# The attention loop of three engines written out for sixteen heads instead of four

## The reference

```python
q = split(x @ Wq.T + bq)
k = split(x @ Wk.T + bk)
v = split(x @ Wv.T + bv)
q_stp = q @ Wqs.T + bqs
k3 = k @ Wks.T + bks
v3 = v @ Wvs.T + bvs
cross_kv = jnp.cross(k3, v3, axis=-1)
scores = (jnp.einsum('bhqd,bhkd->bhqk', q, k) + jnp.einsum('bhqc,bhkc->bhqk', q_stp, cross_kv)) * temp
attn = jax.nn.softmax(scores, axis=-1)
out = jnp.einsum('bhqk,bhkd->bhqd', attn, v)
```

## Time and profile before

| what | us |
|---|---|
| median of 3 runs | 4282.59 |
| lowest and highest | 4281.64 to 4284.22 |
| the profiled execution's own time | 4292.46 |
| its span, first to last instruction | 4290.5 |
| first part of the program | 0 to about 2370 |
| attention: first maxima to last head | 2376.5 to about 3986 |
| feed-forward net | about 3986 to 4290 |
| TensorE busy over the span | 3558.7 (83%) |
| VectorE busy | 3161.5 (74%) |
| ScalarE busy | 2212.4 (52%) |

### The profile page before, as it was taken

How to read it: one execution, slowest core, us unless ns; L and a number is a source line. 1 busy time by engine, 2 the same in 40 slices (tenths; PEclk the granted TensorE clock), 3 DMA queues, 4 the chain that set the end, 5 groups by cost and what they waited for, 6 DMA issues and landing times. The chain is left out here.

```text
span 4290.5 us, 50229 instructions
## 1 busy us (share of the span) xinstructions
PE 3558.7 (83%) x14625; PEld 1618.9 (38%) x14625; DVE 3161.5 (74%) x3753; ACT 2212.4 (52%) x3556; POOL 1513.9 (35%) x1140
## 2 busy tenths in 40 slices
PE   4228778697786987868896799999999999999898
PEld 1015435344353443534553132323222232323565
DVE  5988777887778877777512887878778787878443
ACT  4335544455444544445321277777777777777221
POOL 2977666676666766667611000000000000000110
PEclk7669889898898997988998699999999999999999
DMA  2011212212122121121210200000000000000001
GB/s 93 28 32 44 65 39 77 62 55 72 42 73 65 45 76 45 62 74 50 91 55 25 89 22 17 16 17 24 17 17 16 17 24 17 16 17 19 30 29 34
DMA packets 110769, 183.17 MB, mean 43 GB/s; under 512 B 14495, under 2 KB 84599, under 8 KB 101817
## 3 DMA queue, kind: packets, MB, share of 16 engines
q1 hardware_dynamic: 110521, 180.09, 13.4%
HBM read 153.95 MB, written 26.09 MB: 42 GB/s over the span
## 5 line engine op out<-in xcount | busy, mean ns | idle before, releaser
L1588 DVE TENSOR_REDUCE tile_max<-ps 128x1 f32<-128x1024 f32 x1076 | 1268.3, 1220 | 291.3 <-PE ps L1379 288.6
L1533 ACT ACTIVATE probs<-ps 128x512 f32<-128x512 f32 x2056 | 1119.0, 600 | 493.9 <-PE ps L1393 469.3
L1132 POOL TENSOR_TENSOR h<-h,c_sb 128x512 f32<-128x512 f32 x512 | 696.7, 1391 | 672.3 <-DVE state L937 672.3
L1393 PE MATMUL ps<-qs,ks 101*128 101x512 bf16 x2056 | 714.1, 385 | 1.3
L1379 PE MATMUL ps<-ks,qs 99*128 99x512 bf16 x2152 | 669.6, 393 | 48.9 <-DMA ks<-scratch_kb 41.1
L1143 POOL TENSOR_TENSOR y_sum<-y_sum,h 128x512 f32<-128x512 f32 x512 | 665.2, 1330 | 10.3 <-POOL h L1132 0.5
L930 DVE TENSOR_TENSOR_SCAN h<-decay,state,ps 128x512 f32<-128x512 f32 x512 | 627.5, 1267 | 44.5 <-POOL y_sum L1143 15.1
L498 PE MATMUL ps<-x1T,e_w 128*128 128x512 f32 x1024 | 527.6, 669 | 96.2 <-ACT hid L740 95.8
L1403 PE MATMUL ps<-probs,vh 128*32 128x512 f32 x4096 | 553.5, 613 | 24.6 <-issue 24.6
L1705 POOL COPY vh<-v_all 128x256 f32 (+1 forms) x32 | 12.7, 402 | 1437.2 <-PE ps L1403 1371.7
L518 PE MATMUL ps<-e_w,hid 128*128 128x256 f32 x2048 | 454.1, 380 | 11.3 <-ACT hid L740 7.5
(11 more groups left out here) (172 smaller groups left out, 3115.1 us busy)
## 6 DMA issues: line engine op xcount, KB each, us to landing
e_w<-in_e_w SPq DMA_DIRECT2D x64, 1024.0 KB, 7.0
c_sb<-scratch_c SPq DMA_DIRECT2D x128, 256.0 KB, 3.5
qs<-scratch_q SPq DMA_DIRECT2D x210, 64.0 KB
ks<-scratch_k SPq DMA_DIRECT2D x210, 64.0 KB
scratch_q<-parts SPq DMA_DIRECT2D x16, 384.0 KB, 4.0
scratch_k<-parts SPq DMA_DIRECT2D x16, 384.0 KB, 7.4
xr<-scratch_x SPq DMA_DIRECT2D x10, 512.0 KB, 4.0
xn_tok<-in_x SPq DMA_DIRECT2D x8, 512.0 KB, 4.8
```

What stands on the lines that cost most here:

```text
L1132: last = nc.gpsimd.tensor_tensor(h[:, n % 2, m, :], h[:, n % 2, m, :], c_sb[:, n % C_RING, :], ALU.mult)
L1393: mm(ps[:, S_BANK[i], :], ks[0:K_ALL, j, step * P:(step + 1) * P], qs[0:K_ALL, j, qc * CH:(qc + 1) * CH], start=True, stop=True).then_inc( ...
L1533: fn(probs[:, step % 2, qc, :], ps[:, S_BANK[i], :], ACT.Exp)\
L1588: v.tensor_reduce(tile_max[:, t, half:half + 1], ps[:, slot(side):slot(side) + PAIR, :].rearrange("p a n -> p (a n)"), AX.X, ALU.max).then ...
```

## The change

The body of the loop on TensorE, ScalarE and VectorE is written out for a batch of sixteen heads, so the loop runs twice. On TensorE and ScalarE the body for four heads becomes a function that is called four times in the body. On VectorE the inner hardware loop becomes a Python loop. The order of work on every engine, its waits and its data stay as they are. The loops of GpSimd and SyncE are not touched and still hold four heads.

```diff
-            with pe.Fori(0, heads // ROT) as r:
+            def four_heads(r):
                 for j in range(ROT):
                     u = r * ROT + j
                     base = M_BASE + u * M_PER_HEAD
...
+            with pe.Fori(0, batches) as b:
+                for quad in range(quads):
+                    four_heads(b * quads + quad)
...
-            with act.Fori(0, heads // ROT) as r:
+            def four_heads(r):
                 for j in range(ROT):
                     u = r * ROT + j
                     for step in range(2, KT):
...
+            with act.Fori(0, batches) as b:
+                for quad in range(quads):
+                    four_heads(b * quads + quad)
...
             with dve.Fori(0, batches) as b:
-                with dve.Fori(0, quads) as quad:
+                for quad in range(quads):
                     for j in range(ROT):
                         hd = quad * ROT + j
                         u = b * NH + hd
```

## The result

The changed kernel takes 4240.65 us (median of 4 runs, 4231.37 to 4251.08), the kernel before 4283.27 beside it (4281.64 to 4284.22): a ratio of 0.9902, with a 95% interval of 0.9878 to 0.9925. The forecast was 4244.9, with a range of 4240 to 4253. The profiled execution took 4231.37 us.

A forecast was written before the change was run, and what follows sets the result against it. TensorE was taken to bound the attention, stopping at seven loop returns. Removing six (−38.4 us) and adding register operations (+0.7) gave −37.7: 4254.8 us profiled, 4244.9 as median, with a range of 4240 to 4253.

The forecast's parts named there:

- What bounds the stage: Attention: TensorE sets the pace, busy 46.47 of 46.98 us a head; all other engines stop with it at seven returns.
- Cause of a return's length: TensorE's attention loop: code is fetched anew each pass, so the branch takes 3734 ns in the median, against 220 and 208 elsewhere.
- Six returns: Attention loop, behind heads 4, 8, 12, 20, 24 and 28: removing these returns saves 38.4 us, bounds 34.4 and 40.4.
- The two register operations on TensorE: Between the transposes and `values`, at six places without a branch: a pair adds 0.12 us each, +0.7 us in all.
- The return that stays: Behind head 16: kept by the change; VectorE may need ScalarE's 2.5 us there, costing nothing, at most 2 us.
- last rival's first condition: Attention: the remaining return is cheaper; with this or shorter heads, a few microseconds more go, to 4236; chance 4%.
- the low clock would come back elsewhere: Rival, TensorE in the attention: only the gaps go, the clock falls at other places; 21.1 us saved, 4261.8; chance 5%.
- VectorE's code would come late: Rival, VectorE's 1233-instruction body: it stops for each fetched block, 75 us added, 4320; chance 3%.
- 10 to 20 more packets on queue 14: Sign in the changed kernel's instruction queues: some 10 to 20 packets more on queue 14.
- On queue 8 it was 14 fewer, not 18: Sign on queue 8, taken for TensorE's code: some 18 packets fewer in the changed kernel.
- From profile to median: Whole kernel: returns cost as much in the median run, 9.87 us below the profiled 4292.46, so 4254.8 becomes 4244.9 us.

The follow-up runs named there:

- bodies of 1560 and 1815 instructions: Kernel before with work left out of TensorE's four-head loop: some products with v at 1815 (4273.91 us), also second tiles of maxima pairs at 1560 (4049.47 us).
- the bodies of 1560 and 1320 instructions: Kernel before with work left out of TensorE's four-head loop; at 1320 all products with v but a head's first step go too: 4049.47 and 3993.42 us.
- the repeat: The changed kernel run again with no edit, against the kernel before: 4236.91 us, ratio 0.9886.
- the same 1.42 us of rest: Changed kernel with TensorE waiting for an unneeded GpSimd copy in place of each removed return: 4252.57 us, ratio 0.9939 against the kernel before.

## Why the prediction was right

*What bounds the stage.* That TensorE alone sets the pace and that its returns stop the others was right: with TensorE's code alone changed the attention takes 1462.2 us, with all three engines' 1462.0, and the other engines alone give at most 2.5 us.

*Cause of a return's length.* That the code is fetched anew because the body doesn't stay was argued from two loops. It is shown now by bodies of 1560 and 1815 instructions of the same loop, 0.21 and 3.5 us, without and with packets on TensorE's queue. Where between 1560 and 1815 the limit lies, and what sets it, was not shown. That code is fetched at the return itself is shown by the one packet of queue 8 inside each of the seven long branches. A compare-and-branch that goes back took 207 to 238 ns on TensorE where the body stays (the loops of the first part and of the feed-forward net, and the bodies of 1560 and 1320 instructions), and 3312 to 4065 ns at the seven returns of the kernel before.

*Six returns.* The sum was −38.4 + 0.7 = −37.7 us, and −39.3 were measured over the attention. The six returns that went had cost 38.2 us by the heads behind them. Two other terms were mis-sized by little. The two register operations on TensorE were taken at +0.7 us and cost nothing: heads 5, 9 and 13 take 46.98 to 46.99. The prediction had argued that the sequencer has no lead at this place; the trace shows both operations (37 ns each) while the transposes ahead of them are still running. The return that stays was assumed unchanged and is 1.1 us cheaper, 5.48 in place of 6.58, with half as long at the low clock. That was the last rival's first condition.

*Rivals.* That the low clock would come back elsewhere is refuted by 720 us at 1.00. That VectorE's code would come late is refuted by the 46.98 us of ordinary heads. I had expected 10 to 20 more packets on queue 14 and got 4; that the removed returns of ScalarE took some away is a guess, which no run tests. On queue 8 it was 14 fewer, not 18.

*From profile to median.* I assumed that the parts outside the attention stay the same. In single runs they vary by 20 us, more than the width of my range. With 39.3 us off the median of before (4283.27), 4244.0 would be expected. The first median, 4240.65, lies 0.65 us inside the range, and that of the repeat, 4236.91, lies below it, as does 4239.22 with TensorE alone. So it is the length of the attention that bears the prediction out; that the first median fell inside the range was luck in part. Whether the 3 to 7 us beyond the attention's gain belong to the change is not shown.

## What to carry to other kernels

Look at the sequencer's record of a hardware loop's branch on the engine that bounds the loop, and at its queue of instructions: in this kernel branches of 3.3 to 4.1 us, with 12 packets in a pass, went with a body that didn't stay at the engine, and branches of 0.21 us without a packet with one that did. In the first case either shorten the body until the packets stop, after which a return cost 0.2 us of branch and some 0.4 us in all here, or lengthen it so that there are few returns. In this kernel only the body of the engine that sets the pace mattered. Don't go all the way to constants without looking at where the waits end up, on the other engines too: the work started 0.06 us earlier on TensorE where, of two waits, the instruction itself carried the one that ended last.

## What the runs showed of the hardware

A stop of TensorE cost more than its length when the granted clock fell behind it, which it did in part of the cases: the same 1.42 us of rest was followed by 3.4 us at a clock of 0.51 in one batch of heads (+3.13 us, three times) and by a clock of 1.00 in the other (+1.49 us, three times).

In the kernel without a loop, where an instruction had two waits on constants, a semaphore instruction of its own carried one of them (51 ns on TensorE, 21 on VectorE, 17 on ScalarE). When that one ended last, the work started later: by 0.06 us on TensorE (0.115 against 0.052 behind the reduction's end), 0.07 on VectorE and 0.06 on ScalarE.

The part ahead of the attention varied with the granted clock: the first copy started at 2483.8 us with a clock of 0.87 from 600 to 1800 us, at 2475.3 with 0.88 and at 2463.5 with 0.89. What sets that clock is open.
